# A vision-transformer block on one core: the start-up work of the first images is put in another order

## The reference

```python
p = x -> patches of 16x16x3            # (64, 196, 768)
h = layernorm(p) * ln1_g + ln1_b
h = layernorm(h @ W + b) * ln2_g + ln2_b        # 768 -> 192
h = concat([cls, h], axis=1)                    # 197 tokens
h = h + attention(layernorm(h))   # 12 heads of 64, softmax(q k^T / scale), @ w_out + b_out
h = h + ffn(layernorm(h))         # top-2 of 8 experts give a low-rank term to qkv,
                                  # then attention with 12 heads of 16, @ Wproj + bproj
```

## Time and profile before

| | |
|---|---|
| median of 3 runs | 3128.82 us (3126.43 to 3129.03) |
| the profiled execution | 3129.87 us |
| its span | 3128.1 us |
| PE busy | 2969.7 us, 95% |
| DVE / ACT / POOL busy | 74% / 63% / 19% |
| granted clock of PE, mean | 0.984 |

### The profile page before, as it was taken

How to read it: one execution, slowest core, us unless ns; L and a number is a source line. 1 busy time by engine, 2 the same in 40 slices (tenths; PEclk the granted TensorE clock), 3 DMA queues, 4 the chain that set the end, 5 groups by cost and what they waited for, 6 DMA issues and landing times.

```text
span 3128.1 us, 98362 instructions
## 1 busy us (share of the span) xinstructions
PE 2969.7 (95%) x41624; PEld 2433.5 (78%) x41624; DVE 2330.1 (74%) x5441; ACT 1963.8 (63%) x3777; POOL 594.8 (19%) x859
## 2 busy tenths in 40 slices
PE   4799999999999999999999999999999999999996
PEld 3688788788788778778778778788788778778775
DVE  5677777777777777777777777777777777777773
ACT  2466666666666666666666666666666666666663
POOL 2121121121121121112112111111112112211210
PEclk7899999999999999999999999999999999999998
DMA  4000000000000000000000000000000000000000
GB/s 115 9 21 12 22 19 14 21 15 18 22 16 18 22 14 19 22 13 20 22 13 20 22 13 21 21 12 21 22 12 21 21 12 21 22 12 21 14 4 7
DMA packets 28389, 61.28 MB, mean 20 GB/s; under 512 B 4210, under 2 KB 18389, under 8 KB 27958
## 3 DMA queue, kind: packets, MB, share of 16 engines
q1 hardware_dynamic: 27958, 54.98, 6.0%
HBM read 45.29 MB, written 9.68 MB: 18 GB/s over the span
## 4 chain that ended last, share of the span: by engine, by line
PE 59%; DVE 35%; ACT 3%; issue 3%; DMA 0%; SPq 0%; POOL 0%; DVEq 0%; ACTq 0%
PE psum L676 9%; DVE mx L1090 8%; PE psum L685 8%; PE psum L585 8%; PE psum L602 8%; PE psum L664 4%; PE psum L712 4%; PE psum L612 3%; PE psum L646 3%; DVE st L989 3%; DVE mx L1105 2%; PE psum L715 2%; DVE qk L1184 2%; PE psum L722 2%; DVE o_t L1201 2%
## 5 line engine op out<-in xcount | busy, mean ns | idle before, releaser
L838 ACT ACTIVATE ebufs<-psum 99x788 f32<-99x788 f32 x768 | 592.0, 824 | 58.7 <-PE psum L664 45.4
L513 POOL TENSOR_TENSOR veps<-mv,eps_ln 99x2 f32<-99x2 f32 x256 | 116.0, 453 | 2273.6 <-DVE mv L1019 1341.1
L1105 DVE TENSOR_REDUCE mx<-psum 99x4 f32<-99x788 f32 x384 | 357.5, 973 | 137.6 <-PE psum L629 137.3
L1090 DVE TENSOR_REDUCE mx<-psum 99x4 f32<-99x788 f32 x384 | 362.9, 974 | 52.0 <-PE psum L621 52.0
L602 PE MATMUL psum<-hn_s,qk_w 128*128 128x197 f16 x3840 | 357.3, 250 | 13.9 <-DVE hn_s L1059 7.0
L602 PEld LDWEIGHTS psum<-hn_s,qk_w 128*128 128x128 f16 x3840 | 324.8, 98 | 35.2 <-DVE qk L1184 19.0
L676 PE MATMUL psum<-ebufs,vx 98*32 98x197 f32 (+1 forms) x6144 | 293.7, 331 | 0.0
L585 PE MATMUL psum<-emb_w,xb 128*99 128x193 f32 x1536 | 264.2, 328 | 0.7 <-DVE emb_b L901 0.7
L685 PE MATMUL psum<-out_w,qk 128*99 128x192 f32 x1536 | 263.8, 329 | 0.1
L585 PEld LDWEIGHTS psum<-emb_w,xb 128*99 128x99 f32 x1536 | 248.9, 166 | 2.4 <-DVE emb_b L901 1.0
L676 PEld LDWEIGHTS psum<-ebufs,vx 98*32 98x32 f32 (+1 forms) x6144 | 201.4, 110 | 57.1
(11 more groups left out here) (168 smaller groups left out, 6455.4 us busy)
## 6 DMA issues: line engine op xcount, KB each, us to landing
xb<-x_t SPq DMA_DIRECT2D x64, 591.0 KB, 3.8
out<-h SPq DMA_DIRECT2D x128, 73.5 KB
out<-h SPq DMA_DIRECT2D x64, 0.8 KB
vx<-w_qk SPq DMA_DIRECT2D x2, 384.0 KB, 10.7
qk_sq<-w_emb SPq DMA_DIRECT2D x1, 576.0 KB
vx<-w_qk SPq DMA_DIRECT2D x1, 576.0 KB, 6.9
out_w<-w_out SPq DMA_DIRECT2D x8, 72.0 KB
qk<-w_lora_b SPq DMA_DIRECT2D x1, 480.0 KB
```

The costliest lines, as they stand in the source:

```text
L838: nc.scalar.activation(ebuf[n].rearrange("p e a t -> p e (a t)"), psum[0:TR, b + 2 * half:b + 2 * half + 2, 0:2 * NT], ACT.Exp).then_inc(r ...
L1090: nc.vector.tensor_reduce(mx[s][:, :, 2 * i:2 * i + 2].rearrange("p a e -> p e a"), psum[0:TR, b:b + 2, 0:2 * NT].rearrange("p e (a t) -> ...
L1105: nc.vector.tensor_reduce(mx2[s][:, :, at:at + 2].rearrange("p a e -> p e a"), psum[0:TR, b + 2 * half:b + 2 * half + 2, 0:2 * NT].rearran ...
```

## The change

- `emb_loads` holds three loads instead of seven (weights, gain, bias); image 0's inputs come behind them, and the other four are a group of their own, `norm_loads`, with a semaphore of its own. All of them stay ahead of the loads for QK.
- The squares of image 0 go to `qk[0]` (`xsq_first`), the row of ones to `xss[1]`; ACT and POOL no longer wait for the embedding's constants there. The waits for them stand at the squares of image 1.
- PE makes the product with the ones after image 0's embedding; DVE reads the constants ahead of EMB of image 0 (`constants_of_embedding`), and PE waits for `norm_loads` at T1.
- The split for QK is cut in two: the first 128 rows (`split_rows`) at the head of the start pass, the rest (`weights_of_scores`) behind LC of image 0.
- The split for V stands behind T1 of image 0, and the work for the second block behind T1 of image 1.
- One tile, `late`, holds the raw weights of the second block and later the buffers `o2_t`, `sums2` and `hw_s`, which had tiles of their own. ACT's wait in QK of image 1 is gone.

The diff, cut to its core:

```diff
-        hw_s = two("hw_s", [128, 2, NTP], F16)
-        sums2 = two("sums2", [128, NT])
-        o2_t = two("o2_t", [128, G2, NT])
+        late = sb("late", [128, (G2 + 1) * 2 * NT + 2 * NTP])
+        o2_t = [late[:, G2 * NT * s:G2 * NT * (s + 1)].rearrange("p (m t) -> p m t", m=G2) for s in range(2)]
+        sums2 = [late[:, (2 * G2 + s) * NT:(2 * G2 + s + 1) * NT] for s in range(2)]
...
-        ones = flat(qk[1], 128, 2 * QKV2_RAW, 1, TR)[:, 0]
+        ones = xss[1][:, 0:TR]
+        xsq_first = qk[0][:, 0:KC, :]
...
-        emb_loads = [(emb_raw, w_emb), (ln1_sb, ln1), (ln1b_raw, ln1_bias), (mats_sb, mats), (tok_b, tok_bias),
-                     (tokc, tok_const), (rowc, row_const)]
+        emb_loads = [(emb_raw, w_emb), (ln1_sb, ln1), (ln1b_raw, ln1_bias)]
+        norm_loads = [(tok_b, tok_bias), (mats_sb, mats), (tokc, tok_const), (rowc, row_const)]
...
-            load_group(emb_loads[0:2], emb_loaded)
+            load_group(emb_loads, emb_loaded)
             load(0, 0)
-            load_group(emb_loads[2:], emb_loaded)
+            load_group(norm_loads, norm_loaded)
...
+                        if s == 0 and now.image(p) == 0:
+                            for c in range(KC):
+                                mm = nc.tensor.matmul(psum[0:TR, spare, 0:D], ones, emb_w[:, c, 0:D],
+                                                      start=(c == 0), stop=(c == KC - 1))
+                            mm.then_inc(setup_pe, 1)
...
-                        if now.which == "first" and s == 1 and i == 0:
-                            act.wait_ge(setup_dve, 5)
...
                 if now.which == "start":
-                    weights_of_scores()
-                elif now.which == "first":
-                    weights_of_values()
+                    dve.wait_ge(qk_loaded, 16 * len(qk_loads))
+                    split_rows(qk_w, qk_raw)
...
                     if kind == "EMB":
+                        if s == 0 and now.image(p) == 0:
+                            constants_of_embedding()
...
                         normalise(s, h0[s], hn[s], 0).then_inc(hn_ready[1], 1)
+                        if s == 0 and now.image(p) == 0:
+                            weights_of_scores()
...
+                        if kind == "T1" and now.image(p) == 0:
+                            if s == 0:
+                                weights_of_values()
+                            else:
+                                weights_of_attention2()
...
-                        if now.which == "first" and s == 0 and i == 5:
-                            weights_of_attention2()
```

More of the change, by code:

```diff
@@ L251, in vit_tower @@
         hw = [gl[s][:, :, NE:] for s in range(2)]
-        hw_s = two("hw_s", [128, 2, NTP], F16)
+        late = sb("late", [128, (G2 + 1) * 2 * NT + 2 * NTP])
+        o2_t = [late[:, G2 * NT * s:G2 * NT * (s + 1)].rearrange("p (m t) -> p m t", m=G2) for s in range(2)]
+        sums2 = [late[:, (2 * G2 + s) * NT:(2 * G2 + s + 1) * NT] for s in range(2)]
+        hw_s = [late[:, 2 * (G2 + 1) * NT + NTP * s:2 * (G2 + 1) * NT + NTP * (s + 1)].bitcast(F16).rearrange(
+            "p (v t) -> p v t", v=2) for s in range(2)]
         v2 = two("v2", [TR, 2, H, 2 * DH2])
-        sums2 = two("sums2", [128, NT])
-        o2_t = two("o2_t", [128, G2, NT])
         res = h1
@@ L280, in vit_tower @@
             "p (c f) -> p c f", c=2)
-        lorab_raw = flat(qk[1], 128, 0, 1, QKV2_RAW)
-        bias2_all = flat(qk[1], 128, QKV2_RAW, 1, QKV2_RAW)
+        lorab_raw = late[:, 0:QKV2_RAW].unsqueeze(1)
+        bias2_all = late[:, QKV2_RAW:2 * QKV2_RAW].unsqueeze(1)
         bias2_raw = bias2_all[bias_rows, 0]
-        ones = flat(qk[1], 128, 2 * QKV2_RAW, 1, TR)[:, 0]
+        ones = xss[1][:, 0:TR]
+        xsq_first = qk[0][:, 0:KC, :]
         psum = ctx.enter_context(nc.psum_tensor("psum", [128, 8, 512], F32))
@@ L329, in vit_tower @@
         stored = [sem(f"stored{s}") for s in range(2)]
-        emb_loaded, qk_loaded, v_loaded = sem("emb_loaded"), sem("qk_loaded"), sem("v_loaded")
+        emb_loaded, norm_loaded = sem("emb_loaded"), sem("norm_loaded")
+        qk_loaded, v_loaded = sem("qk_loaded"), sem("v_loaded")
         consts_loaded = sem("consts_loaded")
@@ L476, in _ @@
             nc.gpsimd.memset(ones_col[:], 1.0).then_inc(fills, 1)
-            pool.wait_ge(setup_dve, 2)
             pool.wait_ge(fills, NFILLS)
@@ L494, in body @@
                         wait(pool, now, xsq_ready, p)
-                        link(nc.gpsimd.tensor_tensor(xsq[:, 0:3, :], xsq[:, 0:3, :], xsq[:, 3:6, :], ALU.add))
-                        link(nc.gpsimd.tensor_tensor(xsq[:, 0, :], xsq[:, 0, :], xsq[:, 1, :], ALU.add))
-                        nc.gpsimd.tensor_tensor(xss[s][:], xsq[:, 0, :], xsq[:, 2, :], ALU.add
+                        sq = xsq_first if s == 0 and now.image(p) == 0 else xsq
+                        link(nc.gpsimd.tensor_tensor(sq[:, 0:3, :], sq[:, 0:3, :], sq[:, 3:6, :], ALU.add))
+                        link(nc.gpsimd.tensor_tensor(sq[:, 0, :], sq[:, 0, :], sq[:, 1, :], ALU.add))
+                        nc.gpsimd.tensor_tensor(xss[s][:], sq[:, 0, :], sq[:, 2, :], ALU.add
                                                 ).then_inc(xss_ready[1], 1)
@@ L522, in _ @@
         def _(pe):
+            spare = next(b for b in range(8) if b not in [BANK[(k, s, 0)] for k in ("EMB", "T1") for s in range(2)])
             pe.wait_ge(emb_loaded, 16 * len(emb_loads))
             for c in range(KC):
-                nc.tensor.matmul(psum[0:TR, 1, 0:D], ln1b_raw[:, c, :], emb_raw[:, c, :],
+                nc.tensor.matmul(psum[0:TR, spare, D:2 * D], ln1b_raw[:, c, :], emb_raw[:, c, :],
                                  start=(c == 0), stop=(c == KC - 1))
@@ L529, in _ @@
             pe.wait_ge(setup_dve, 1)
[L530 to L534, removed]
             SPLIT = ((0, 0), (0, 1), (1, 0))
@@ L568, in body @@
                         continue
-                    if now.which == "first" and s == 0:
-                        if kind == "QK" and i == 0:
+                    if s == 0 and now.image(p) == 0:
+                        if kind == "T1":
+                            pe.wait_ge(norm_loaded, 16 * len(norm_loads))
+                        elif kind == "QK" and i == 0:
                             pe.wait_ge(setup_dve, 3)
@@ L750, in _ @@
             act.wait_ge(fills, NFILLS)
-            act.wait_ge(setup_dve, 2)
             nc.scalar.preload_act_table_set("natural_log_exp_and_others")
@@ L771, in body @@
                         act.wait_ge(x_loaded[s], (now.image(p) + 1) * 16)
-                        wait_free(act, now, sq_users, squares_used)
-                        nc.scalar.activation(xsq, xb[s][:], ACT.Square).then_inc(xsq_ready[1], 1)
+                        first = s == 0 and now.image(p) == 0
+                        if not first:
+                            wait_free(act, now, sq_users, squares_used)
+                            if now.image(p) == 0:
+                                act.wait_ge(setup_dve, 2)
+                        nc.scalar.activation(xsq_first if first else xsq, xb[s][:], ACT.Square
+                                             ).then_inc(xsq_ready[1], 1)
                     elif kind in ("T1", "T2"):
@@ L898, in _, with constants_of_embedding @@
                                     ).then_inc(setup_dve, 1)
[L899 to L903, removed]
+            dve.wait_ge(fills, NFILLS)
+            def constants_of_embedding():
+                spare = next(b for b in range(8) if b not in [BANK[(k, s, 0)] for k in ("EMB", "T1") for s in range(2)])
+                dve.wait_ge(norm_loaded, 16 * len(norm_loads))
+                dve.wait_ge(setup_pe, 1)
+                nc.vector.tensor_copy(emb_cs[:], psum[0:TR, spare, 0:D])
+                nc.vector.tensor_tensor(emb_b[:], tok_b[:, 0, :], psum[0:TR, spare, D:2 * D], ALU.add
+                                        ).then_inc(setup_dve, 1)
+                dve.wait_ge(setup_dve, 2)
             def split_weights(dst, raw, by=WS):
@@ L913, in _, with split_rows @@
             splits = [0]
+            def split_rows(w, raw):
+                return split_weights(lambda v: w[:, v], raw[:, 0])
             def split_packed(w, raw):
-                split_weights(lambda v: w[:, v], raw[:, 0])
                 nc.vector.tensor_scalar(w[:, 2], raw[:, 1], WS, None, ALU.mult).then_inc(setup_w, 1)
@@ L937, in weights_of_scores @@
             def weights_of_scores():
-                dve.wait_ge(qk_loaded, 16 * len(qk_loads))
                 split_packed(qk_w, qk_raw)
@@ L949, in weights_of_values @@
                 dve.wait_ge(v_loaded, 16 * len(v_loads))
+                split_rows(v_w, v_raw)
                 a = split_packed(v_w, v_raw)
```

1 line of the change is left out of this document (removed).

## The result

| | before | changed |
|---|---|---|
| median | 3128.08 us (3126.21 to 3129.5, 6 runs) | 3116.24 us (3113.6 to 3117.66, 6 runs) |
| ratio | | 0.996, 95% interval 0.9949 to 0.9971 |
| the profiled execution, its span | 3129.87, 3128.1 us | 3115.51, 3113.7 us |

The change gains 11.8 us, 0.4%. Run once more beside before, the same file gave 3116.22 us against 3128.4, ratio 0.9959 (0.9945 to 0.9973). The forecast was 3114.3 us in a range of 3110.5 to 3119.5. It was right in direction and in its main mechanism, and 1.9 us too low in the number. The gain itself was put at 14.5 us, 2.7 too high; part of that does not show in the time, because the forecast started from a median of 3128.82 us and before has 3128.08 over six runs.

A forecast was written before the change was run, and what follows sets the result against it. PE bounds the full pipeline, so the prediction counted how much earlier the start-up chain brings PS of image 1: 3.9 + 11.3 - 0.7 = 14.5 us, giving 3114.3 us from 3128.82, range 3110.5 to 3119.5.

The forecast's parts named there:

- Joint 1: Start-up to LC of image 0: earlier loads give only cover; with the split's second half moved, LC ends 4.82 us earlier.
- Joint 2: LC to QK of image 0: rest of QK's split replaces V's split before `hn_s`; QK starts 3.9 us earlier.
- Joint 3: Image 1's norms before the second block's weights: T1 follows PV, QK of image 1 starts 11.3 us earlier.
- Joint 4: The 50 second-block instructions ahead of S of image 1 exceed their cover; PS comes 0.7 us later against QK.
- Both signs against the forecast: PS of image 1 later than 98.5, or PS to the end differing from 3019.1 us by more than 2.
- the block only changes places: Rival: the 50 instructions cost as much ahead of S as ahead of LA; gain 3.5 to 7 us; chance 0.08.
- joint 1 pays nothing: Rival: PE's products or POOL's adds hold EMB, LC no earlier or 2 us; gain 10 to 11.5 us; chance 0.10.
- Slower, by the packed buffers: Rival: buffers at odd offsets in `late` slow each image; 0.23 us per image eats the 14.5 us; chance 0.02.
- More: Rival: QK of image 1 runs faster and the block is shorter; gain 16.5 to 18 us; chance 0.12.

The follow-up runs named there:

- the embedding first: Changed kernel with all of QK's split, and DVE's wait for QK's weights, put behind LC of image 0; 3110.88 us.
- the second execution: The changed kernel run once more, unchanged, to see how far its marks move from one execution to the next; 3116.22 us.
- the block cut as well: Changed kernel with QK's split behind LC and the last 11 instructions of the second block's weights behind M.2 of image 0; 3106.96 us.

## Why the prediction was right, and where it was off

*Joint 1* was right. DVE's start did not move but for the load (0.44 us later in this profile); LC ended at L + 12.00 where I had L + 12.06. That the early loads buy little but cover was shown by putting them back (0.74 us at QK0) and, from the other side, by the embedding first (5.4 us).

*Joint 2* was right in its sum of about 3.9 us, with 3.7 measured (QK0 - L 22.69 before, 18.99 after), and wrong in what it credits. I booked 4.8 us to the split's rest going out of the way ahead of LC and took off 1 us behind it. The experiments split the gain otherwise: V's move earns 3.1, and moving the rest of QK's split costs 0.7 on balance. The remaining 1.3 I put down to image 0's early squares; this is read from the rows, and no run undoes the squares alone. In their old place POOL's adds lengthened the split, which took 8.20 us from L to the mean; in one piece with POOL idle, and with the constants added, it takes 7.04. The turns of DVE and POOL that I took for a cost inside the new place also stood in the old one. Behind LC they were larger than I let them be: POOL's second add went ahead of the waiting DVE, so the stretch from LC to QK0 took 6.99 us, not 6.7.

*Joint 3* was right: T1 follows PV, and PE's queue is next in line. From `neg` to QK1 I had 10.5 us; it took 11.05, of 21.85 before. The 0.5 us go with the clock of PE's products of V and ST, 0.63 in the first 7 us; in the second execution it was 0.75 and the stretch took 10.45.

*Joint 4* was right that the block is too long for its cover. S came 12.14 us behind QK1, not 12.9. POOL's adds had 1.4 us of work left when the block began at 80.19, close to the 1.3 foreseen, but cost it only 0.5 us: it took 12.2 where it had taken 11.7. PS came 14.88 behind QK1, not 15.5.

The cover itself had changed, which the forecast's 9.8 us and 2.4 us left out. They were measured in before, where QK of image 1 began at a clock of 0.50, behind PE's 10.16 us of idle time. In the changed kernel that gap is gone and the same 60 products, at 1.00, are through in 5.92 us instead of 8.17:

```profile
94.20 8.17 PE L602 MATMUL psum<-hn_s,qk_w 128*128 128x197 f16 x60 [2.13 <-DVE hn_s L1059]
```
```profile
84.30 1.88 PE L612 MATMUL psum<-hn_s,qk_w 128*128 128x197 f16 x20 [0.47 <-ACT qk L806]
86.95 0.82 ACT L811 ACTIVATE qk<-psum 128x788 f32<-128x788 f32 x1
```

The first row is before, the other two the changed kernel. ACT's last read for S now ends 7.5 us behind QK1, so S waits 4.6 us for the block alone, and PE is free for PS 12.6 us behind QK1 instead of 14.8. The time that QK won came back as PE's 2.26 us of idle time.

*The step that was left out* is what the idle time before PS does to PE. I priced PS's lateness, 0.7 us, but not a longer gap nor the clock behind it: PS took 1.65 us instead of 0.93 and N moved by another 0.7. With joints 2 to 4 and 0.3 us from N to M this closes the account: 3.26 - 0.12 (QK0 to `neg`) + 10.80 - 0.07 - 0.72 - 0.34 = 12.81 us, as at M, against 14.5 forecast. In the second execution, where the clock stayed up, M had moved by 14.6. But that one is a single execution too; the medians stand at 11.8 and 12.2, so the agreement of 14.6 with the forecast is luck in part. Both signs against the forecast stayed away: PS of image 1 started at 95.14, ahead of 98.5, and from it to the end it is 3018.56 us, within 2 us of 3019.1.

Of the rivals, "the block only changes places" is out (putting it back costs 9.6 us), and so is "joint 1 pays nothing". "Slower, by the packed buffers" is out by M, which keeps its distance, and by line 1227, the old L1201:

```profile
L1227 DVE TENSOR_TENSOR late<-psum,late x192: 327/353/366, 160.0 to 3105.8; 128x197 f32<-128x197 f32 x192
```

"More" was right that QK of image 1 runs faster, and the block took that gain back. One thing was not tried: what DVE and POOL take turns over was not measured alone; it is shown only by the same instructions with and without the other engine beside them.

## What to carry to other kernels

In a start-up of one pass, look at each engine's first long wait and ask whether what it stands for is needed by the next thing in its queue; here the best order put the work that could already run in front of the wait, and was worth 5 us, more than cutting the block (about 2) or the early loads (0.7). One-off work belongs behind the step that feeds the other engines, cut so that each piece fits the idle time there, and it may need a buffer of its own to go there at all. A cover is measured under the conditions of the old kernel: when a change removes an idle gap ahead of it, the work in it can get faster and the cover shorter. Compare distances between marks, not instants: a load's landing moved everything by up to 2 us from run to run.

## What the runs showed of the hardware

- An instruction of DVE that waited for POOL was not served between two adds of POOL's: L940 took 3.82 us behind LC, from 32.78 on, while L508 and then L501 ran until 34.99, and 1.75 us when POOL was idle. It took 3.82 or 3.83 us in all seven profiles with this order.
- In two more kernels the one of the two engines that started later was the slow one. With the embedding first, L940 started ahead of POOL's L501 and ran its 1.75 us; with the block cut as well, L501 started ahead and L940 took 2.94:

```profile
29.47 1.75 DVE L940 SCALAR_TENSOR_TENSOR qk_w<-vx,qk_w 64x1536 f16<-64x1536 f32 x1
29.89 2.62 POOL L501 TENSOR_TENSOR qk_sq<-qk_sq 128x591 f32<-128x591 f32 x1 [2.94 <-ACT qk_sq L786]
```
```profile
29.87 1.46 POOL L501 TENSOR_TENSOR qk_sq<-qk_sq 128x591 f32<-128x591 f32 x1 [2.38 <-ACT qk_sq L786]
30.01 2.94 DVE L940 SCALAR_TENSOR_TENSOR qk_w<-vx,qk_w 64x1536 f16<-64x1536 f32 x1
```

- The granted clock after nearly the same idle time on PE, 2.26 and 2.39 us, was 0.50 in one execution and 1.00 in another of the same file.
- The load of QK's weights, issued from 6.0 to 6.8 us on, released DVE anywhere from 19.4 to 21.7 us in the ten profiles in which DVE waited for it; the later issues were not always the later landings (6.81 with 19.83, 6.05 with 21.20).
